# Routed adapters on one core: weights laid out by the host and fetched in one transfer each, and one piece of VectorE's work moved within a step

## The reference

```python
h = einsum(x, W_down[role]) + b_down[role]        # 1024 -> 512
h = gelu(h)
y = x + einsum(h, W_up[role]) + b_up[role]        # 512 -> 1024
out = (y - mean(y)) * rsqrt(var(y) + 1e-5) * gamma[role] + beta[role]
```

## Time and profile before

| What | Value |
|---|---|
| median of 3 runs | 2792.06 us (2791.12 to 2796.57) |
| the profiled execution: its own time | 2793.15 us |
| its span (first to last instruction) | 2791.3 us |
| mean granted clock of TensorE | 0.991 |
| share of the span that the DMA engines' main queue took | 63.0% |
| chain that ended last | PE 70%, issue 10%, DVE 10%, DVEq 3%, ACT 2%, DMA 2% |

### The profile page before, as it was taken

One profiled execution on the slowest core, in us unless ns is written; L12 is line 12 of the kernel. 1 busy time (PEld: TensorE's weight loads), 2 busy tenths in 40 slices (PEclk: granted clock), 3 DMA queues, 4 the chain that ended last, 5 costly groups with the idle time before them and its releaser, 6 DMA issues.

```text
span 2791.3 us, 57347 instructions
## 1 busy us (share of the span) xinstructions
PE 2697.3 (97%) x11714; PEld 2204.6 (79%) x11714; DVE 2198.4 (79%) x3350; ACT 1698.8 (61%) x2905; POOL 1337.6 (48%) x1050
## 2 busy tenths in 40 slices
PE   7999999998999999999989999999889999999997
PEld 5888888877788888888778787878677877878785
DVE  5777776778777776777898888888788888888887
ACT  4565665656566665656656566656555566666565
POOL 1455555544555555555434444444344444444445
PEclk9999999999999999999999999999999999999999
DMA  6666666667665666666776565666666666666664
GB/s 193 206 215 198 211 206 207 209 214 222 207 225 198 213 205 208 208 205 210 218 217 207 195 219 191 213 201 204 201 208 208 204 206 196 203 201 210 198 210 149
DMA packets 366212, 573.67 MB, mean 206 GB/s; under 512 B 40992, under 2 KB 240800, under 8 KB 365728
## 3 DMA queue, kind: packets, MB, share of 16 engines
q1 hardware_dynamic: 365728, 569.61, 63.0%
HBM read 364.97 MB, written 204.47 MB: 204 GB/s over the span
## 4 chain that ended last, share of the span: by engine, by line
PE 70%; issue 10%; DVE 10%; DVEq 3%; ACT 2%; DMA 2%; SPq 1%; POOL 1%; ACTq 0%; POOLq 0%
PE pD L519 36%; PE bX L531 19%; PE bZ L531 14%; DVE xt L909 3%; DVEq L228 2%; DVE hl L891 2%; DVE xt L932 1%; DVE wul L810 1%; DVE xl L869 1%; DVE xt L901 1%; ACT pC L689 1%; ACT xh L631 1%; DMA cbd<-in_bd 1%; DMA htok<-hg 1%; DVE xT L862 0%
## 5 line engine op out<-in xcount | busy, mean ns | idle before, releaser
L465 POOL TENSOR_TENSOR xt<-xt,cgb 128x1024 f32<-128x1024 f32 x258 | 643.2, 2493 | 423.8 <-ACT xt L697 423.8
L519 PE MATMUL pD<-wdh,xh 128*128 128x512 f32 x2080 | 813.6, 391 | 12.3 <-DVEq L853 10.2
L519 PE MATMUL pD<-wdl,xh 128*128 128x512 f32 x2080 | 812.3, 391 | 0.0
L519 PE MATMUL pD<-wdh,xl 128*128 128x512 f32 x2080 | 811.9, 390 | 0.0
L697 ACT ACTIVATE xt<-xt,rstd 128x1024 f32<-128x1024 f32 x258 | 296.7, 1150 | 457.5 <-POOL rstd L451 371.1
L519 PEld LDWEIGHTS pD<-wdh,xh 128*128 128x128 f32 x2080 | 392.5, 189 | 97.0 <-DVEq L853 7.1
L932 DVE SCALAR_TENSOR_TENSOR xt<-xt,nmean,cgb 128x1024 f32<-128x1024 f32 x260 | 462.4, 1778 | 0.0
L519 PEld LDWEIGHTS pD<-wdl,xh 128*128 128x128 f32 x2080 | 392.6, 189 | 82.1
L519 PEld LDWEIGHTS pD<-wdh,xl 128*128 128x128 f32 x2080 | 392.4, 189 | 82.3
L531 PE MATMUL bX<-wuh,hh 128*128 128x512 f32 x1040 | 412.2, 396 | 42.7 <-DVE xt L901 20.0
L689 ACT ACTIVATE pC<-xt,nmean 128x512 f32<-128x512 f32 x520 | 359.8, 692 | 137.6 <-DVE nmean L917 78.0
(11 more groups left out here) (98 smaller groups left out, 3747.9 us busy)
## 6 DMA issues: line engine op xcount, KB each, us to landing
xq<-in_xB SPq DMA_DIRECT2D x130, 512.0 KB, 3.5
htok<-hg SPq DMA_DIRECT2D x260, 256.0 KB, 2.8
hq<-htok SPq DMA_DIRECT2D x1040, 64.0 KB, 2.2
xt<-in_x SPq DMA_DIRECT2D x130, 512.0 KB, 4.2
mid<-xt SPq DMA_DIRECT2D x130, 512.0 KB, 3.6
xq<-mid SPq DMA_DIRECT2D x520, 128.0 KB, 3.1
xt<-mid SPq DMA_DIRECT2D x130, 512.0 KB, 4.1
out<-xt SPq DMA_DIRECT2D x128, 512.0 KB, 2.7
```

Source lines behind the costliest of these rows:

```text
L465: eng.tensor_tensor(xt[:, k, :], xt[:, k, :], cgb[:, 1, :], ALU.add).then_inc(s_o, 1)
L519: last = eng.matmul(pD[e][:, :], a[:, e, 128 * k:128 * k + 128], w[:, k, :], start=False, stop=(k == 7 and n == 2), skip_group_check=True)
```

## The change

The host lays both weight arrays out as they lie on chip: partition by partition, 16 KB in a row. Then:
- The first down weights are fetched in four quarters of 128 partitions, each with a semaphore of its own; ScalarE waits for one quarter at a time (`first_down`, `high_wd`).
- Later down weights are one transfer of 128 partitions, issued behind the rows xt. The bias is issued ahead of the rows, where weights and bias stood. ScalarE waits for the whole transfer before the first quarter.
- Up weights are one transfer each. The first one is issued by ScalarE, in `begin(0)` behind `high_h(i - 2, 0)`; the later ones by SP where they were.
- VectorE takes factors 0 and 1 (with the difference in cbu, and the words s_wu[0] and s_cb) behind the fifth eviction and `low_x`, where they stood ahead of the fourth eviction.

```diff
-        s_rd = [sem(f"s_rd{k}") for k in range(2)]
+        s_rd0 = [sem(f"s_rd0{k}") for k in range(4)]
+        s_rd = sem("s_rd")
...
+        def fetch_up(eng, row):
+            eng.dma_start(rwu[:, :, :, :, :].rearrange("p g c n k -> p (g c n k)"),
+                          Wu[row, :, :].rearrange("a p n -> (a p) n")).then_inc(s_ru, 16)
...
+            def first_down(row):
+                eng.wait_ge(f_rd, pd.next() + 1)
+                for q in range(4):
+                    eng.dma_start(rwd[:, 2 * q:2 * q + 2, :].rearrange("p k n -> p (k n)"),
+                                  Wd[row, :, 2 * K * q:2 * K * q + 2 * K].rearrange("a p n -> (a p) n"))\
+                       .then_inc(s_rd0[q], 16)
+
             def down_weights(p):
-                down_row(adapter(p))
-
-            def down_row(row):
-                c = pd.next()
+                row, c = adapter(p), pd.next()
                 eng.wait_ge(f_rd, c + 1)
-                for h in range(2):
-                    for a in range(4):
-                        r = 256 * a + 128 * h
-                        eng.dma_start(rwd[32 * a:32 * a + 32, 4 * h:4 * h + 4, :],
-                                      Wd[row, r:r + 128, :].rearrange("a (k i) n -> (a i) k n", i=32))\
-                           .then_inc(s_rd[h], 16)
+                eng.dma_start(rwd[:, :, :].rearrange("p k n -> p (k n)"), Wd[row, :, :].rearrange("a p n -> (a p) n"))\
+                   .then_inc(s_rd, 16)
...
-            def next_down(p):
-                down_weights(p)
-                down_bias(p)
...
                 eng.wait_ge(f_ru, c + 1)
-                for g in range(2):
-                    for a in range(4):
-                        r = 128 * a + 64 * g
-                        eng.dma_start(rwu[32 * a:32 * a + 32, g, :, :, :].rearrange("p c n k -> p c (n k)"),
-                                      Wu[row, r:r + 64, :].rearrange("a (k i) n -> (a i) k n", i=32)).then_inc(s_ru, 16)
+                fetch_up(eng, row)
...
+            pu.next()
             eng.wait_ge(s_first, 1)
...
-            down_row(row)
+            first_down(row)
...
                 load_h(v, 1)
-                if i.first():
-                    up_weights(i)
                 if not (i + 1).first():
-                    when_new(eng, i + 1, next_down)
+                    when_new(eng, i + 1, down_bias)
                 load_rows(w, 0)
                 load_rows(w, 1)
+                if not (i + 1).first():
+                    when_new(eng, i + 1, down_weights)
...
             def high_wd(p, c, q):
                 count(eng, s_Db, p + -1, 4, q + 1)
-                eng.wait_ge(s_rd[q // 2], c * 64 + 64)
+                if p.first():
+                    eng.wait_ge(s_rd0[q], 16)
+                else:
+                    eng.wait_ge(s_rd, c * 16)
...
                 high_h(i + -2, 0)
+                if i.first():
+                    eng.wait_ge(f_ru, 1)
+                    fetch_up(eng, bass.ds(eng.value_load(c_q[0:1, 0:1], min_val=0, max_val=5), 1))
                 when_new(eng, i + -3, take_wu_2)
...
                 low_h(w, 1)
-                when_new(eng, w, take_wu_0)
-                ready(w, s_wu[0])
-                ready(w, s_cb)
                 last_onto(u, 4, bZ, 0, 1, 3)
                 scale(u + -1, 1)
                 last_onto(u, 5, X, 1, 1, 2)
                 low_x(i + 1, 0)
+                when_new(eng, w, take_wu_0)
+                ready(w, s_wu[0])
+                ready(w, s_cb)
                 last_onto(u, 6, bZ, 0, 0, 1)
```

More of the change, by code:

```diff
@@ L598, in take_wu_0 @@
                 count(eng, s_P, p + -1, 7, 2)
-                eng.wait_ge(s_ru, c * 128 + 128)
+                eng.wait_ge(s_ru, c * 16 + 16)
                 high_wu(0, b11)
@@ L1022 @@
         "itok": itok_B_1_2,
-        "Wd": np.concatenate([L0_cond_W_down, L1_cond_W_down]),
+        "Wd": np.concatenate([L0_cond_W_down, L1_cond_W_down]).reshape(6, 4, 8, 32, K).transpose(0, 1, 3, 2, 4)
+                .reshape(6, 128, 8 * K),
         "bd": np.concatenate([L0_cond_b_down, L1_cond_b_down]),
-        "Wu": np.concatenate([L0_cond_W_up, L1_cond_W_up]),
+        "Wu": np.concatenate([L0_cond_W_up, L1_cond_W_up]).reshape(6, 4, 4, 32, H).transpose(0, 1, 3, 2, 4)
+                .reshape(6, 128, 4 * H),
         "bu": np.concatenate([L0_cond_b_up, L1_cond_b_up]),
```

## The result

The changed kernel took 2801.21 us (median of 7 runs, 2799.76 to 2804.45), the kernel before 2793.40 beside it (7 runs, 2790.94 to 2796.57). The ratio is 1.0031, 95% interval [1.0019, 1.0043]: slower, by 0.3%. The prediction was 2785.5, between 2774 and 2793, with 11% for slower, so it had the wrong sign.

The account below looks back on a forecast made before the run. TensorE, busy 97% of the span, was taken as the bound, so only its standing time could be won. Start -6.5, down -0.4 and up -0.2 made -7; the median was put at 2785.5 us, range 2774 to 2793.

Parts of the forecast that it names:

- Down group, -0.4: First waits at the three adapter changes: bias wait becomes a weights wait, -0.4 us in sum, best bound -3.
- 2.10 MB / 414 = 5.1 us: Later down weights' transfer time at 414 GB/s, counted from first data, itself put 1 us after issue.
- a landing above 9 us: Sign that the forecast is wrong: later down weights take over 9 us, not 6 to 7, from issue to landing.
- the division by it, 5.9 us: Down weights priced at the skill's 358 GB/s: 5.9 us, each change 0.8 us later, forecast 2788.
- third rival: Late down weights decide: long rows run at 225 GB/s, +12.6 us over three changes, 2800 us in all; 10%.
- Up group, -0.2 with +3 as the worst: Later waits at the three adapter changes: product 5's wait moves to products 0 and 2; -0.2 us, bounds -13 and +3.
- nothing leaves VectorE: Up group: the same VectorE instructions still stand ahead of the eviction that product 2 of the next step needs.
- 8.9 against 8.9: Up group: VectorE's time from low_h to the sixth eviction at the third change, 8.9 us both new and old.
- Start, -6.5: First step: first matmul 2.5 us earlier, product 2 at 62.0 not 68.06; -6.5 us, bounds -8 and -1.
- the case I left for the range: Start: a shorter pause keeps TensorE's clock up, saving 1.7 us on the first 12 matmuls; product 2 then -7.7.
- that rival: Start is given back: a longer VectorE and ScalarE chain and late blocks leave -1 in all, 2791 us; 25%.
- Flag asked twice on SP, 0: SP's second flag query, some 0.5 us in each of 130 steps, hides behind the stores' wait; bound +1.

Follow-up runs that it names:

- E5: Changed kernel with later down weights in four quarters, a flag each, ahead of the rows, and VectorE's old order: 2775.19 us, ratio 0.9937 to the kernel before.
- E11: E5 with the later down weights in two halves, a flag each, instead of quarters: 2777.80 us, ratio 0.9949 to the kernel before.
- E2: Changed kernel with the later down weights' one transfer issued directly behind the bias, ahead of the rows: 2790.45 us, ratio 0.9993 to the kernel before.
- E3: Changed kernel with later down weights in four quarters, a flag each, ahead of the rows; VectorE's new order kept: 2782.99 us, ratio 0.9966 to the kernel before.
- E7: Changed kernel with later down weights in four quarters, a flag each, still behind the rows: 2788.63 us, ratio 0.9985 to the kernel before.
- E6: Kernel before with only VectorE's new order (factors 0-1 behind the fifth eviction and low_x): 2801.18 us, ratio 1.0026 to the kernel before.
- E1: Changed kernel with VectorE's old order put back (factors 0-1 ahead of the fifth eviction): 2793.98 us, ratio 1.0006 to the kernel before.
- E12: E5 with the first up weights issued by SyncE in the kernel before's place, as one transfer, not by ScalarE: 2779.14 us, ratio 0.9952 to the kernel before.
- E4: Changed kernel with later down weights as eight 32-partition pieces ahead of bias and rows, and VectorE's old order: 2784.09 us, ratio 0.9973 to the kernel before.
- E10: E3 with VectorE taking factors 0-1 directly behind the eviction of product 4, ahead of the scaling: 2777.33 us, ratio 0.9949 to the kernel before.
- E8: Kernel before with only the down-projection's bias issued ahead of the eight weight pieces: 2788.37 us, ratio 0.9982 to the kernel before.
- E9: E3 with VectorE taking factors 0-1 between the sixth eviction and the next low_x: 2781.92 us, ratio 0.9964 to the kernel before.

## Why the prediction was wrong

**Down group, -0.4: wrong, at +8.3, and this decides the sign.** The order of events was right: the bias wait went, one for the weights came, SP passed the rows first (issue 4.6 us behind the bias, against 4.1 in the working). The term that failed is the landing: "2.10 MB / 414 = 5.1 us" and 1 us to the first data, 6.1 to 6.6 in all. Measured were 8.4, 10.1 and 9.8; the prediction's own sign of being wrong, a landing above 9 us, showed in T2 and T3. The seeds come 2.2, 3.8 and 2.7 us later, 8.7 together; the matmuls lost 8.3. Two things were missing from the term.

The first is the traffic beside the load. The windows of T2 show it (length, busy PE, PEld, DVE, ACT, POOL, clock, DMA share, GB/s):

```profile
1335.00:1337.00 2.00, 2.00 (x11) 1.65 (x10) 2.00 (x2) 0.57 (x2) 0.86 (x1) 1.00 1.14 461
1337.00:1339.00 2.00, 2.00 (x11) 1.65 (x10) 2.00 (x4) 0.00 (x0) 0.00 (x0) 1.00 0.98 377
1339.00:1341.00 2.00, 2.00 (x11) 1.65 (x10) 0.51 (x3) 0.00 (x0) 0.00 (x0) 1.00 0.97 336
1341.00:1343.00 2.00, 1.97 (x9) 1.31 (x7) 0.00 (x0) 0.00 (x0) 0.00 (x0) 1.00 0.95 244
1343.00:1345.00 2.00, 0.00 (x0) 0.00 (x0) 0.00 (x0) 0.00 (x0) 0.00 (x0) 1.00 0.93 361
```

The engines move 356 GB/s over these ten microseconds, 3.6 MB, and only 2.1 of them are weights. The rest was issued ahead of the weights (rows) or behind them (the transfers of 1330 to 1350, KB each, us to landing):

```profile
rwd<-in_Wd SPq DMA_DIRECT2D x1, 2048.0 KB, 10.1
xt<-in_x SPq DMA_DIRECT2D x2, 512.0 KB, 4.3
mid<-xt SPq DMA_DIRECT2D x1, 512.0 KB, 10.3
xq<-mid SPq DMA_DIRECT2D x4, 128.0 KB, 8.5
```

I had divided the weights by a rate for all transfers, and the load never had that rate to itself.

The second is time that doesn't go with the bytes. Ahead of the rows, where less shares the engines, the first quarter (0.5 MB) still takes 4.6 to 5.3 us from issue to landing in E5, the first half (1 MB) 5.1 to 6.0 in E11 and the whole (2.1 MB) 7.8 to 9.0 in E2; the bias, 0.26 MB, takes 3.5 us in T1 and T2 of the changed kernel. Taking off the bytes at 414 GB/s leaves 2.5 to 4 us in each case, an estimate of mine from these times. The working had 1 us. With 2.5, the least of these, in its place it gives 7.6 us and not 6.1 to 6.6, so 1.0 to 1.5 us of each miss are of this kind, and the rest of it (some 1, 2.5 and 2 us) goes with the traffic. What the fixed part consists of stays open.

In the Trainium skill, "DMA: Bandwidth & Descriptors" (Specifications) gives 358 GB/s for a core. The 356 here fit it, while E3 has 380 from 1336 to 1346, so it isn't a ceiling of this traffic; and the division by it, 5.9 us, fails in the same way as mine. In the Trainium skill, "SBUF — State Buffer" (The DMA setup-cost knee) has the rule to coalesce DMA-bound transfers into the largest single one possible. Here the single one is slower than four, by 7.5 us (E2 against E3) and 12.8 us (the changed kernel against E7): the time to the first usable quarter counted, not the rate. The Trainium skill's page "Perfetto Trace Analysis" (DMA Optimizations) holds that splitting transfers may let some start sooner. E7's trace agrees for the use of the data: the first conversion starts 5.1 to 5.6 us behind the issue.

My third rival (2800, 10%) had the late weights and their point of decision, "some 9 us per transfer", but for a wrong reason. It took the 128 long rows to run at 225 GB/s, which is 9.3 us from the first data on, and E2's land 7.8 us behind their issue in T3. That its 2800 is so near 2801 is luck: it had +12.6 for the down groups (+8.3 measured) and nothing for the order (+3.8 in the up groups).

**Up group, -0.2 with +3 as the worst: wrong in size.** That product 5 would cease to wait and products 0 and 2 would wait instead was right, and so was "nothing leaves VectorE". The step that failed is the sum "8.9 against 8.9": it took the factors at 2.3 us behind the scaling's 3.3, as if only one instruction could meet GpSimd. Both do. VectorE of the changed kernel in T3, and of the kernel before at the eviction for which both sums stand:

```profile
2058.55 3.31 DVE L937 SCALAR_TENSOR_TENSOR xt<-xt,nmean,cgb 128x1024 f32<-128x1024 f32 x1
...
2063.52 4.26 DVE L815 TENSOR_TENSOR wul<-rwu,wuh 128x1024 fp32r<-128x1024 f32 x2
...
2068.82 0.69 DVE L914 SCALAR_TENSOR_TENSOR xt<-bZ,xt 128x512 f32<-128x512 f32 x1 [0.43 <-DVE cbu L832]
```

```profile
2063.09 0.69 DVE L909 SCALAR_TENSOR_TENSOR xt<-bZ,xt 128x512 f32<-128x512 f32 x1
```

From the fourth eviction (2057.94) to the sixth it is 10.9 us after; from the factors (2053.84) to the sixth it was 9.25. These are the 1.7 us that T3's up group lost. Over the three changes the price is 6.1 us in E6 and 3.8 in the changed kernel; between E3 and E5 it is 6.7.

**Start, -6.5: right, at -7.3.** The first matmul was put at 18.05 (17.92). The clock was kept (granted clock 1.00 from 18 to 26), the case I left for the range; for it I had -7.7. From the start of xl (46.88) to product 2 (60.76) it took 13.9 us, and the working has 9.44 + 3.2 + 1.2 = 13.8. The net price of the order at this place is less, 2.8 us in E1, for the factors cost time in the old order too. ScalarE's early issue (2.5 us, E12 against E5) and this price cancel: the changed kernel has product 2 7.3 us early, and E12, with neither, 7.4. The start isn't given back, so that rival falls.

**Flag asked twice on SP, 0: small, as said.** Between T1's up group and T2, from 754 to 1316, lie some 26 steps with the second flag and without new weights, and the changed kernel lost 0.1 us in them. Its "rest" of 2.8 us is for 2.1 us behind T3's up group. E1 has 1.5 in all, E7 0.5, both with the second flag, and E2 and E3, without it, nothing. It stays open whether this is scatter; the runs of one kernel differ by more (E2: 2787.89 to 2793.42).

**The sum.** The medians of the first group, with the changed kernel put in by its ratio (2800.4), split its 8.6 us so: start -7.7 (before to E4), one transfer behind the rows +9.9 (E4 to E1), the new order +6.4 (E1 to after). The parts were put at -6.5, -0.4 and -0.2, with the order's 2.8 us at the start counted in the first.

## What to carry to other kernels

Before merging the transfers of a load, ask who waits for its first part: with a flag per quarter the consumer starts after the first 0.5 MB, with one flag after all of it and after whatever shares the engines meanwhile. Halves did nearly as well here (E11). When you price a load, take a measured time from issue to landing of one of its kind, and not its bytes by a rate alone. Put the small transfer that gates first, but don't let bulk that nobody awaits pass the load that is awaited. A wait seen on the busiest engine may be the shadow of a chain on another: moving the shadow wins nothing (E10), and a new order that lets work on that chain stand behind a wait or beside a blocking neighbour costs time (2.8 us at the start in E1, 1.5 to 2.4 us at each change in E6).

## What the runs showed of the hardware that I had not expected

TensorE's clock behind a wait is not the same from one trace to the next. E1 and E5 come to product 4 of the first pair in the same way (VectorE's old order, the same first weights), with the same wait of 2.83 us. The timeline of TensorE behind that wait, in E5:

```profile
66.72 0.50 PE L534 MATMUL bX<-wuh,hh 128*128 128x512 f32 x1 [2.83 <-DVE xt L907]
...
67.53 0.40 PE L534 MATMUL bX<-wuh,hh 128*128 128x512 f32 x1
67.76 0.39 PE L534 MATMUL bX<-wul,hh 128*128 128x512 f32 x1
```

and in E1:

```profile
66.48 0.53 PE L530 MATMUL bX<-wuh,hh 128*128 128x512 f32 x1 [2.83 <-DVE xt L906]
...
67.67 0.63 PE L530 MATMUL bX<-wuh,hh 128*128 128x512 f32 x1
68.09 0.63 PE L530 MATMUL bX<-wul,hh 128*128 128x512 f32 x1
```

In E1 the matmuls start 0.43 us apart, at the lower of the two clock levels (granted clock 0.50 from 67 to 69), in E5 0.23 (1.00). Nine traces have this wait of 2.8 us. In E1, E3, E8, E9, E10 and E12 the 30 matmuls behind it took 8.5 to 8.6 us, in E4, E5 and E11 6.9 us, so the lower level cost 1.6 us. The other five traces wait only 1.2 us there and lose nothing. Product 2 shows the same: behind a wait of 3.0 us the changed kernel, E2 and E7 fell to the lower level for a while (mean granted clock 0.57, 0.57 and 0.66 from 62 to 66), while E3 and E12 stayed at 1.00. Each kernel has one trace, so it isn't shown whether the kernel or the execution decides. But an account made from one trace is uncertain by that much for each such wait, and only the medians settle what is smaller.
